# Two-layer graph network on one core: a second tile per three turns fetched row by row in the first layer, and twelve node numbers per register load

## What is computed

```python
h = relu(layernorm(x));  h_s, h_v = h[:, :64] @ lin1_ws, h[:, 64:] x lin1_wv
w = silu(edge_attr_64 @ fc_w1) @ fc_w2          # first layer: 224 weights per edge
es, ev = h_s[src], h_v[src]                     # the gather: one row of 160 floats per edge
m = [w1*es*e0, w4*dot(ev,e1), w2*es*e1, w3*ev*e0, w5*cross(ev,e1)]
agg = segment_sum(m, dst);  x = x + gate(agg @ lin2 + h @ sc)
# second layer: the same gather of relu(layernorm(x))[src], products with e0, e1 alone,
# segment_sum, then weights, relu, and x + (x + relu(...))
```

## Time and profile before

| what | us |
|---|---|
| median of 3 runs | 1938.24 (1938.19 to 1938.62) |
| the profiled execution | 1939.32, its span 1937.5 |
| POOL busy | 1408.5 (73% of the span) |
| PE busy | 1791.9 (92%) |
| DVE busy | 1371.9 (71%) |
| ACT busy | 174.6 (9%) |
| gathers on POOL | 1472, mean 947 ns |
| rows fetched one by one | 2304 by SP, 1152 by ACT |

### The profile page before, as it was taken

How to read it: one execution, slowest core, us unless ns; L and a number is a source line. 1 busy time by engine, 2 the same in 40 slices (tenths; PEclk the granted TensorE clock), 3 DMA queues, 4 the chain that set the end, 5 groups by cost and what they waited for, 6 DMA issues and landing times.

```text
span 1937.5 us, 55467 instructions
## 1 busy us (share of the span) xinstructions
PE 1791.9 (92%) x16896; PEld 1559.4 (80%) x16896; DVE 1371.9 (71%) x2793; ACT 174.6 (9%) x402; POOL 1408.5 (73%) x1505
## 2 busy tenths in 40 slices
PE   6989889898989899898975999999999999999998
PEld 4767666676767676676654899999999999999998
DVE  5878787878787878787778556666565665656654
ACT  5100001010010001010122000000000000000000
POOL 1777777777777777777755777777777777777774
PEclk9999999999999989899986999999999999999999
DMA  6333333434334343434323333233333323333233
GB/s 239 103 101 104 103 104 103 104 93 109 98 103 105 103 104 103 105 92 114 102 70 82 77 73 77 72 77 73 77 75 73 76 72 76 73 76 76 73 77 91
DMA packets 110902, 179.67 MB, mean 93 GB/s; under 512 B 30046, under 2 KB 78460, under 8 KB 110460
## 3 DMA queue, kind: packets, MB, share of 16 engines
q0 software_dynamic: 70656, 120.68, 26.1%
q1 hardware_dynamic: 35288, 53.34, 8.7%
q10 hardware_dynamic: 4644, 2.19, 0.5%
HBM read 169.95 MB, written 6.14 MB: 91 GB/s over the span
## 4 chain that ended last, share of the span: by engine, by line
POOL 49%; PE 23%; issue 18%; DVE 4%; DMA 3%; ACTq 2%; DVEq 1%; POOLq 0%; ACT 0%
POOL g L704 49%; PE w_ps L1003 12%; PE sums L992 4%; PE sums L1013 2%; DMA g<-node_table,src 2%; ACTq L612 1%; DVE work L858 1%; PE sums L1003 1%; PE sums L988 1%; PE w_ps L956 1%; DVE work L852 1%; PE w_ps L481 1%; PE sums L460 1%; PE hid_ps L942 1%; ACTq L609 0%
## 5 line engine op out<-in xcount | busy, mean ns | idle before, releaser
L704 POOL DMA_INDIRECT g<-node_table,src x1472 | 1394.0, 947 | 479.7 <-issue 464.3
L1003 PE MATMUL w_ps<-H,work 128*128 128x160 f32 x2900 | 405.5, 300 | 1.5 <-issue 1.5
L1003 PEld LDWEIGHTS w_ps<-H,work 128*128 128x128 f32 x2900 | 399.2, 191 | 1.9 <-issue 1.9
L858 DVE TENSOR_TENSOR work<-w_ps,g 128x384 f32<-128x384 f32 (+3 forms) x693 | 297.8, 457 | 87.6 <-DMA g<-node_table,src 47.7
L956 PE MATMUL w_ps<-fc_sb,work 64*128 64x224 f32 x1612 | 238.0, 394 | 90.8 <-DVE work L852 78.4
L877 DVE STREAM_TRANSPOSE turned<-sums 128x160 f32<-128x160 f32 x232 | 79.3, 342 | 306.9 <-PE sums L1013 201.8
L988 PEld LDWEIGHTS sums<-work,sel 128*32 128x32 f32 x6448 | 203.6, 114 | 112.9 <-issue 70.1
L956 PEld LDWEIGHTS w_ps<-fc_sb,work 64*128 64x128 f32 x1612 | 172.7, 199 | 137.8 <-DVE work L852 104.8
L806 DVE TENSOR_TENSOR sel<-mixed,sh 128x896 f32<-128x896 f32 x232 | 251.4, 1084 | 26.6
L988 PE MATMUL sums<-work,sel 128*32 128x160 f32 x6448 | 255.5, 311 | 0.0
L992 PE MATMUL sums<-g,sel 128*128 128x160 f32 x1612 | 237.5, 301 | 6.6 <-DMA g<-node_table,src 4.9
(11 more groups left out here) (85 smaller groups left out, 650.1 us busy)
## 6 DMA issues: line engine op xcount, KB each, us to landing
g<-node_table SPq DMA_DIRECT2D x2304, 0.6 KB
feat<-edge_feat_dram SPq DMA_DIRECT2D x60, 512.0 KB
g<-node_table,src POOLq DMA_INDIRECT x1472
g<-node_table ACTq DMA_DIRECT2D x1152, 0.6 KB
named<-src_rows_dram SPq DMA_DIRECT2D x30, 192.0 KB
X<-x_dram SPq DMA_DIRECT2D x5, 400.0 KB, 7.1
node_table<-H SPq DMA_DIRECT2D x5, 400.0 KB, 2.7
named<-src_rows_dram SPq DMA_DIRECT2D x30, 64.0 KB
```

Source lines behind the costliest of these rows:

```text
L704: nc.gpsimd.indirect_dma_start(out=g[:, slot(p, u, j), :], out_offset=None, in_=table[layer], in_offset=bass.IndirectOffsetOnAxis(ap=src[: ...
L858: nc.vector.tensor_tensor(blocks(at), w[:, :, 2 * S_CH + j * V_CH:2 * S_CH + (j + 1) * V_CH].unsqueeze(2).to_broadcast([P, n, m, V_CH]), r ...
L1003: last = nc.tensor.matmul(found_at[:, i, 0:D], match[layer][i][:, t, :], H[:, t, :], start=(t == 0), stop=(t == NT - 1))
```

## The change

In the first layer ACT now fetches a tile row by row too, the last tile of group 3 of every turn p = 1, as it did in the second layer already. POOL leaves that tile out. `SHARES` is the table of the second layer for both layers (what stood in the first entry wasn't used before): 12 rows behind each stage, 8 behind the eleventh, none behind the twelfth. `AT_ONCE` rises from 8 to 12, for SP and ACT in both layers, so that a share of 12 takes one register load and not two (8 and 4).

```diff
-ROW_TILES = (1, 2)
+ROW_TILES = (2, 2)
 PARTS = (48, 48, 32)
-SHARES = ((0, 12, 12, 12) + (12,) * 4 + (12, 12, 12, 8), (12,) * 8 + (12, 12, 8, 0))
-AT_ONCE = 8
+SHARES = ((12,) * 8 + (12, 12, 8, 0),) * 2
+AT_ONCE = 12
```

## The result

The changed kernel takes 1926.79 us (median of 5 runs, 1926.05 to 1929.59) against 1938.24 (5 runs, 1936.81 to 1938.81): 11.45 us less, a ratio of 0.9942 with a 95% interval of 0.9932 to 0.9953. The prediction was 1927.2. The profiled execution took 1926.79 us, its span is 1925.0.

What follows compares the result with a forecast made beforehand. POOL's issue of gathers was taken to bound the first layer, PE and POOL together the second. Nine gathers less: 1938.24 - 11.27 = 1927.0, with 0.2 off the gain for the layer's end 1927.2 us; range 1926.0 to 1934.

Steps and rivals of the forecast that it cites:

- Nine gathers at 1.252 us on the path: First layer on POOL: nine tiles moved to ACT save 11.27 us, all on the path if the consumers keep up.
- A load of 12 numbers, 0.87 us, a share 5.9: ACT, first layer: one load of 12 takes 0.87 us, bounds 0.72 and 1.06; 12 rows with it take 5.9 us.
- rival (c): ACT's load of 12 costs 0.2 us per number, share 7.5 us, slip 9.6, time 1955 us; chance 0.02.
- The consumers' own period, 94.1: First layer: three turns of 30.4 us plus 2.9 for the loop's turn-over, 94.1 us against POOL's 98.9.
- Slip 3.0 us per period: ACT's rows delay consumers 1.0 us in turn p = 0, none in p = 1, up to 2.0 at the loop's turn-over.
- POOL keeps setting the pace: First layer: consumers' period with slip is 97.1 us, under POOL's 98.9, so POOL's gathers still set the pace.
- rival (a): First layer: consumers partly become the bound at slip of 6.0 to 7.4 us per period; 1929 to 1937 us; chance 0.13.
- Rival (b), slower: ACT's silu of the next group 0 holds PE; share 7.1 us gives slip 8.0, 1942.7 us; chance 0.08.
- The second layer: PE and POOL bind together, so no gain: 0, bounds 0 and 1.6 us; its start moves with the first layer's end.

Runs made afterwards that it cites:

- POOL alone with its part: Changed kernel, but in the first layer ACT brings each row-fetched tile with one DMA of wrong rows instead of 128; 1927.29 us, ratio 0.9944.
- once4_b: Changed kernel with 4 node numbers per register load for ACT in the first layer; 1983.39 us, ratio 1.0225.

## Why the prediction was right, and which steps were off
- **Nine gathers at 1.252 us on the path:** right, 11.26 us between first and last gather. POOL alone with its part gave 0.9944, the whole change 0.9942.
- **A load of 12 numbers, 0.87 us, a share 5.9:** the loads on ACT now have a median of 0.96 us. A share takes 5.85 us in the median of 80, 5.73 to 6.26, from the start of ACT's instruction ahead of it to its last DMA, as the prediction measured it. The bounds held, and rival (c) is out. The Trainium skill ("Runtime: NRT & Kernel Launch", "Instruction fetch mechanics") puts a register load at about 200 ns per register, which would make this one 2.4 us, an estimate. Its figure is off by more than a factor of two for these loads, which read SBUF:

```profile
L609 SPq TENSOR_LOAD <-by_row x198: 710/998/1073, 45.7 to 1833.1; - x198
L609 ACTq TENSOR_LOAD <-by_row x198: 717/959/1110, 80.9 to 1881.4; - x198
```

- **The consumers' own period, 94.1:** the turn of 30.4 us was right to 0.05. The turn-over was read from one of eight and came out 1.3 us short of the mean of six: 95.3.
- **Slip 3.0 us per period:** mis-sized, it is 4.1, and its parts were further off than the sum. In the turn p = 0 it was 1.0 and is 1.1 to 1.6: the clock was taken as full behind PE's wait for the silu, and in part of the periods it isn't. In the turn p = 1 it was 0, and here a step was missing: I followed the silu to PE, but not the rows to DVE. The tile that they make up lands 1.7 us after DVE wants it, in nearly every period. Together these two are 3.3 us. The loop's turn-over was given up to 2.0 us; all that is left for it and the rest of those turns is 0.8. Too little in one place was in part made up by too much in the other.
- **So "POOL keeps setting the pace" was wrong in the middle of the layer:** 97.1 was reckoned, 99.4 came, against POOL's 98.9. The time held because of the other half of that part: a lag is lost only if the end doesn't make it good. 8 x 0.5 = 4 us of lag stood against 9.9 us that DVE had waited in the last turns. It was closer than the prediction says: of the 4.8 + 1.2 = 6.0 us per period from which rival (a) was to begin, 99.4 - 94.1 = 5.3 were used, not 3.0. That a margin of 0.7 us was left, with two parts of the slip mis-sized, was luck.
- **Rival (b), slower:** the mechanism is there and its price was far too low. A share of 7.1 us was put at 8.0 us of slip and 1942.7 us; `once4_b` has that share, 107.5 - 95.3 = 12.2 us of slip and 1983.4 us. Slip doesn't grow in step with the share: PE's idle time and the slower matmuls behind it add up (22 of 26 times, 10 of 25 in the changed kernel), while the late tile grew little.
- **The second layer:** no change, as forecast; PE's small waits for tiles fetched by row, 1.6 us, went, and 4.7 us for gathered rows came in their place between 1090 and 1900 us (2.9 before). The end moved with its start.

## What to carry to other kernels
Where a fast engine runs ahead of slow consumers, price the transfer of work by both periods, the leader's and the followers': the gain is the leader's as long as the followers' period stays within it plus what the end can make good. Follow a moved piece of work to both of its readers, the instruction queued behind it and the consumer of its result: here the same rows, ending one stage later, turned a gain of 11 us into a loss of 51. And expect a wait of TensorE to cost more than its length: behind waits of some 2 us its matmuls were slower in 10 of 25 cases, behind some 3 us in 22 of 26.

## What the runs showed that was not expected
The same kernel takes 1938 us in some runs and 3067 or 3115 in others, with PE idle for nothing visible in the midst of straight rows of matmuls. In the slower ones 107 indirect gathers fewer shortened the kernel by 274 us (3115.03 to 2840.75), 2.6 us each, twice what a gather costs POOL; in the others it was 51 us, 0.5 each, until the consumers' pace was reached. Why PE stands idle there, and why fewer gathers help so much, none of these runs tells.
